# Attention in a fused two-layer kernel: lags between scores, transposed scores and weighted values, and the places of the work that rides along

## The chip, the cores and the metric

The kernel runs on one core of one Trainium2 chip. The time is the device time of one execution in microseconds, as the median of several runs. A core has five engines with queues of their own: TensorE (PE in the profile; PEld are its weight loads), VectorE (DVE), ScalarE (ACT), GpSimd (POOL) and SyncE (SP, which here only issues DMAs). Each queue is worked off in the order in which it was written, and engines wait for one another by semaphores.

## The reference, cut to what matters

The reference is two transformer-like layers over x of shape 2 x 512 x 512. Layer 0 is an attention of 32 heads (8 groups of keys and values, 4 heads to a group, head size 16) behind a modulated layer norm, then a gated low-rank feed-forward part; layer 1 has weights in 4-bit codes with scales. The change touches the attention of layer 0 and what is computed beside it:

```python
k = jnp.repeat(k, NREP, axis=2)
v = jnp.repeat(v, NREP, axis=2)
scores = jnp.einsum('bihd,bjhd->bhij', q, k) * SCALE
scores = jnp.where(causal, scores, jnp.finfo(scores.dtype).min)
attn = jax.nn.softmax(scores, axis=-1)
out = jnp.einsum('bhij,bjhd->bihd', attn, v)
```

and, of layer 1, the decoding of the weights, `w = NF4[codes]`, multiplied by a scale for each block of 64; q, k and v of layer 1 are added, so that one sum of three decoded matrices is needed.

## The kernel before

**Attention.** A unit is one tile of 128 queries for the 4 heads of one group: B x GROUPS x TB = 64 units, four to a group (unit n is tile n % 4 of group n // 4), and because of the causal mask the tiles need 1, 2, 3 and 4 blocks of 128 keys. For each unit:

- `scores(n)` (TensorE, L1607 and the mask L1609): two pairs of heads into PSUM banks 0 to 3. There is one set of these banks, so a pair is written only when the maxima of the same pair of the unit before were taken (semaphore `s_mx`).
- the maxima (VectorE, `reduce_max`, L1295) into one of two tiles of `MX`; a tile is overwritten only when GpSimd has used it (`s_dg`).
- the diagonal (GpSimd, L731): the maxima times an identity, written under the queries in the stack `QS`, so that the next product subtracts them.
- `transposed(n)` (TensorE, L1622, mask L1625): the scores again, keys on the partitions, less the maxima, one matmul per key block, into three banks in turn. A block needs the exponential of the third block before it.
- the exponential (ScalarE, L879) into ten tiles `PT`.
- `weighted(n)` (TensorE, L1639): the values and the denominators into bank 7, 4 matmuls per block, in pairs of units.

`scores(n)`, `transposed(n - 2)` and, at odd n, `weighted` of units n - 5 and n - 4 stand in one loop over n. When a group is complete, its bank 7 is copied by ScalarE (`copy_even`, L566) for even groups and by VectorE (`copy_odd`, L1215 and L1217) for odd ones. Each pair of groups is then finished on VectorE: `swap_sums` (L1223), two halves of a reciprocal (`invert`, L1227) and `divide` (L1232); ScalarE rounds the heads (`round_heads`) and VectorE splits them (`split_heads`, L1239).

**Work that rides along.** During attention six pieces of layer 1's codes are decoded. A piece has four steps, placed on units by `step_at(n)`: in each eight units the slots 2, 4 and 6. Steps 0 to 2 are curves on ScalarE (L837, four for a piece: two at step 0) and a sum on VectorE (L1157); step 3 is the `fold` on ScalarE (L846). ScalarE does the curves three units ahead of their slot (`ride(n + 3)`), the fold at it. GpSimd then scales the piece in two halves (`scale_half`, L687) one and two units behind the fold's unit, and adds it (`add_half`, L701) three and four units behind.

**SyncE's queue** (`load_stack`, L552 and L558): for each group twelve DMAs bring queries and keys into one of three stacks, each set behind a wait for the last transposed scores of the third group before. `load_piece` (codes L494, scales L503) stands between them, at groups 0, 5, 8, 11 and 14. The order of all this is written out by hand in the tables at the top of the file.

## Time and profile before

| what | us |
|---|---|
| median of 3 runs (952.17 to 954.70) | 953.95 |
| the profiled execution, its own time | 952.0 |
| its span from the first to the last instruction | 950.1 |
| TensorE busy | 877.9 (92%) |
| VectorE busy | 693.6 (73%) |
| ScalarE busy | 533.1 (56%) |
| GpSimd busy | 189.5 (20%) |
| mean granted TensorE clock | 0.976 of full speed |

The span is that of the profiled execution; its own time has the start and the end around it as well. Busy shares are means over stages with different limits, so the stage of the change has to be read by itself. In a row, "idle before" is the time in which an engine did nothing just before an instruction, and behind the arrow stands what ended it. Starts of TensorE's instructions are recorded and their ends are modelled, so durations are best read from one start to the next.

### The profile page before, as it was taken

The numbers are of one execution on the slowest core, as the hardware profiler recorded it, in microseconds if no ns is written. First come the engines' busy times: TensorE is split into PE (matmuls) and PEld (weight loads), VectorE is DVE, ScalarE is ACT, GpSimd is POOL, SyncE is SP. The second block draws the span as 40 slices with busy tenths as digits, with TensorE's granted clock in tenths as the row PEclk, the third lists the DMA queues.
The fourth block names the chain that finished last, engine by engine and source line by source line (L and its number), as shares of the span: only waits on it lengthen the run. The fifth ranks groups of instructions, "written<-read, shape, count | busy, mean of one in ns | idle before, by whom it ended". The sixth has DMA issues, their size and how long they took to land.

```text
span 950.1 us, 13799 instructions
## 1 busy us (share of the span) xinstructions
PE 877.9 (92%) x5224; PEld 693.3 (73%) x5224; DVE 693.6 (73%) x892; ACT 533.1 (56%) x707; POOL 189.5 (20%) x197
## 2 busy tenths in 40 slices
PE   2799999999988889898999999999988999999996
PEld 1567667666667668686888888788866888888885
DVE  3835698888888768778677777587887866667842
ACT  3313667657654434486666657477727766666830
POOL 3002555666557213300000000000040000000004
PEclk9798999999898999999999999999999999999998
DMA  9588565655535103105233333133312333332202
GB/s 309 171 243 152 67 109 69 113 101 66 103 78 179 34 12 105 51 22 147 83 106 103 102 99 113 46 105 95 111 45 67 111 104 97 99 101 67 67 1 89
DMA packets 40610, 93.59 MB, mean 99 GB/s; under 512 B 7000, under 2 KB 10072, under 8 KB 40544
## 3 DMA queue, kind: packets, MB, share of 16 engines
q1 hardware_dynamic: 36416, 87.35, 36.6%
q10 hardware_dynamic: 4128, 5.36, 1.7%
q8 instruction: 42, 0.69, 0.3%
q14 instruction: 24, 0.20, 0.1%
HBM read 77.98 MB, written 2.11 MB: 84 GB/s over the span
## 4 chain that ended last, share of the span: by engine, by line
PE 75%; DVE 9%; issue 5%; POOL 4%; ACT 3%; DMA 2%; SPq 1%; POOLq 0%; DVEq 0%; ACTq 0%
PE PS L1509 15%; PE PS L1510 14%; PE PS L1511 14%; PE PS L1815 5%; PE PS L1814 5%; PE PS L1813 5%; PE PS L1607 4%; PE PS L1639 2%; PE PS L1622 2%; DVE MX L1295 2%; POOL QS L731 2%; DMA WM<-in_WM 1%; POOL X L715 1%; PE PS L1531 1%; DVE ACC L1157 1%
## 5 line engine op out<-in xcount | busy, mean ns | idle before, releaser
L837 ACT ACTIVATE PL<-CODE 128x1024 f32<-128x1024 int32 x200 | 201.9, 1057 | 60.3 <-DVE ACC L1157 55.7
L1509 PE MATMUL PS<-HH,WRH 128*128 128x512 f32 x448 | 176.7, 394 | 11.2 <-DVE HL L1116 4.7
L1510 PE MATMUL PS<-HH,WRL 128*128 128x512 f32 x448 | 175.6, 392 | 0.0
L1511 PE MATMUL PS<-HL,WRH 128*128 128x512 f32 x448 | 175.6, 392 | 0.0
L715 POOL TENSOR_TENSOR X<-X,SCR 128x512 f32<-128x512 f32 x32 | 42.6, 1343 | 560.2 <-DVE SCR L1142 560.1
L1157 DVE SCALAR_TENSOR_TENSOR ACC<-PL,ACC 128x1024 f32<-128x1024 f32 x100 | 123.1, 1231 | 8.4
L879 ACT ACTIVATE PT<-PS 128x512 f32<-128x512 f32 x160 | 85.5, 602 | 67.3 <-PE PS L1622 45.1
L1295 DVE TENSOR_REDUCE MX<-PS 128x2 f32<-128x256 f32 (+3 forms) x128 | 100.5, 820 | 29.4 <-PE PS L1609 14.8
L1509 PEld LDWEIGHTS PS<-HH,WRH 128*128 128x128 f32 x448 | 84.9, 189 | 31.2 <-issue 6.3
L731 POOL TENSOR_TENSOR QS<-ident,MX 64x256 fp32r<-64x256 f32 x128 | 93.6, 732 | 66.6 <-DVE MX L1295 60.0
L1511 PEld LDWEIGHTS PS<-HL,WRH 128*128 128x128 f32 x448 | 84.8, 189 | 18.0
L1510 PEld LDWEIGHTS PS<-HH,WRL 128*128 128x128 f32 x448 | 85.0, 190 | 17.0
L1607 PE MATMUL PS<-KS,QS 128*128 128x128 f32 (+3 forms) x256 | 83.5, 387 | 7.8 <-DVE MX L1295 5.9
L1451 DVE TENSOR_TENSOR HID<-SG,PS 128x512 f32<-128x512 f32 x56 | 37.2, 684 | 69.1 <-PE PS L1511 44.6
L1813 PE MATMUL PS<-WRH,HH 128*128 128x512 f32 x216 | 84.1, 389 | 0.0
L1815 PE MATMUL PS<-WRH,HL 128*128 128x512 f32 x216 | 84.0, 389 | 0.0
L1814 PE MATMUL PS<-WRL,HH 128*128 128x512 f32 x216 | 84.0, 389 | 0.0
L1607 PEld LDWEIGHTS PS<-KS,QS 128*128 128x128 f32 x256 | 50.3, 196 | 30.0 <-DVE MX L1295 18.6
L1157 DVE SCALAR_TENSOR_TENSOR ACC<-PL 128x1024 f32<-128x1024 f32 x50 | 61.5, 1229 | 11.4 <-ACT PL L837 11.3
L846 ACT ACTIVATE ACC<-ACC 128x1024 f32<-128x1024 f32 x50 | 52.9, 1058 | 29.7 <-DVE ACC L1157 29.7
L1622 PE MATMUL PS<-QS,KN 128*128 128x512 f32 x160 | 57.1, 439 | 13.2 <-ACT PT L879 8.2
L1609 PE MATMUL PS<-maskR,padR 128*128 128x128 f32 x256 | 59.1, 240 | 0.0
(225 smaller groups left out, 1528.2 us busy)
## 6 DMA issues: line engine op xcount, KB each, us to landing
CODE<-in_CODES SPq DMA_DIRECT2D x50, 512.0 KB, 3.5
SCALE<-in_SCALES SPq DMA_DIRECT2D x100, 256.0 KB, 4.0
WM<-in_WM SPq DMA_DIRECT2D x12, 1024.0 KB, 5.9
QS<-FH SPq DMA_DIRECT2D x32, 128.0 KB, 4.1
QS<-FL SPq DMA_DIRECT2D x32, 128.0 KB, 5.1
X<-in_X ACTq DMA_DIRECT2D x2, 1024.0 KB, 12.3
GAB<-gates SPq DMA_DIRECT2D x4, 512.0 KB, 3.8
out_x<-X ACTq DMA_DIRECT2D x8, 256.0 KB, 2.0
```

The lines of the kernel that those rows point to most:

```text
L731: nc.gpsimd.tensor_tensor(QS[64:P, q % STACKS, :, ic * P + 64 * half:ic * P + 64 * half + 64], ident[rows, rows].unsqueeze(1).to_broadcast ...
L837: nc.scalar.activation(PL[:, n % 3], CODE[:, p % 2], ACT.Prelu, scale=scale, bias=bias, alpha=alpha).then_inc(s_plane, 1)
L879: nc.scalar.activation(block_of(n, jc)[:].rearrange("p h i -> p (h i)"), PS[:, 4 + done % 3], ACT.Exp, scale=HD ** -0.5).then_inc(s_exp, 1)
L1157: nc.vector.scalar_tensor_tensor(acc, PL[:, at_plane % 3], CAPS[i], rest_of, ALU.min, ALU.add).then_inc(s_used, 1)
L1295: nc.vector.reduce_max(MX[:, n % 2, 2 * pair:2 * pair + 2], PS[:, 2 * pair:2 * pair + 2, 0:w], AX_X).then_inc(s_mx, 1)
L1509: nc.tensor.matmul(dst, lh, rh, start=start and k == 0, stop=False)
L1510: nc.tensor.matmul(dst, ll, rh, start=False, stop=False)
L1511: ins = nc.tensor.matmul(dst, lh, rl, start=False, stop=stop and k == KC - 1)
L1607: nc.tensor.matmul(PS[:, h, 0:(ic + 1) * P], QS[:, q % STACKS, h, ic * P:(ic + 1) * P], KS[:, q % STACKS, 0:(ic + 1) * P], start=True, sto ...
L1813: nc.tensor.matmul(dst[t], hh, wh, start=(n == 1 and k == 0), stop=False, skip_group_check=True)
L1814: nc.tensor.matmul(dst[t], hh, wl, start=False, stop=False, skip_group_check=True)
L1815: ins = nc.tensor.matmul(dst[t], hl, wh, start=False, stop=last and n == 1, skip_group_check=True)
```

## The change

It changes places, not work. The transposed scores follow the scores by three units (`TURN`) instead of two, the weighted values of two units by six and five, at even n. The maxima have three tiles instead of two. The slots of the decoding are 0, 2 and 4 instead of 2, 4 and 6. On ScalarE a curve is done alone, five units (the first of a piece: seven) ahead of its slot, and the fold one unit behind it, all behind the unit's exponentials and ahead of the copy of an even group. GpSimd's scale halves come five and six units behind the fold's slot, its sums seven and eight. The copies, the swap, the inversions and the division on VectorE move to other units. Codes and scales are loaded at tables of their own.

```diff
-PIECES_AT = {0: (0, 1), 5: (2,), 8: (3,), 11: (4,), 14: (5,)}
+CODES_AT = {0: (0, 1), 4: (2,), 6: (3,), 9: (4,), 11: (5,)}
+SCALES_AT = {0: (0, 1), 5: (2,), 8: (3,), 11: (4,), 14: (5,)}
+MAXIMA = 3
+TURN = 3
-ROUND_AT = {41: 0, 46: 1, 49: 2, 54: 3, 58: 4, 60: 5, 63: 6}
+ROUND_AT = {41: 0, 46: 1, 49: 2, 54: 3, 58: 4, 61: 5, 63: 6}
...
-    slots = (2, 4, 6)
+    slots = (0, 2, 4)
...
-                    scale_at[n + 1 + half] = p, half
+                    scale_at[n + 5 + half] = p, half
-                        add_at[(n + 3 if p < 4 else B * GROUPS * TB - 3) + half] = p, half
+                        add_at[(n + 7 if p < 4 else B * GROUPS * TB - 3) + half] = p, half
...
-                if step_at(n) and step_at(n)[1] < STEPS - 1:
-                    curves(*step_at(n))
+                if step_at(n + 7) and step_at(n + 7)[1] == 0:
+                    curve(step_at(n + 7)[0], 0)
+                if step_at(n + 5) and step_at(n + 5)[1] < STEPS - 1:
+                    p, s = step_at(n + 5)
+                    curve(p, s + 1)
+                if step_at(n - 1) and step_at(n - 1)[1] == STEPS - 1:
+                    fold(step_at(n - 1)[0])
-            for n in range(3):
+            for n in range(-7, 0):
                 ride(n)
...
+                ride(n)
                 if n % 8 == 5:
                     copy_even(act, n // TB - 1)
-                ride(n + 3)
-                if step_at(n) and step_at(n)[1] == STEPS - 1:
-                    fold(step_at(n)[0])
...
-                    if n >= 2:
-                        dve.wait_ge(s_dg, 2 * (n - 1))
+                    if n >= MAXIMA:
+                        dve.wait_ge(s_dg, 2 * (n - MAXIMA + 1))
...
-                if pair_at(n, 4) is not None:
-                    copy_odd(pair_at(n, 4))
                 if pair_at(n, 5) is not None:
-                    swap_sums(pair_at(n, 5))
-                for half, unit in enumerate((5, 6) if n >= 60 else (7, 8)):
+                    copy_odd(pair_at(n, 5))
+                if pair_at(n, 14) is not None:
+                    divide(pair_at(n, 14))
+                if pair_at(n, 6) is not None:
+                    swap_sums(pair_at(n, 6))
+                for half, unit in enumerate((6, 7) if n >= 62 else (8, 12)):
                     if pair_at(n, unit) is not None:
                         invert(half)
-                if pair_at(n, 7 if n >= 60 else 9) is not None:
-                    divide(pair_at(n, 7 if n >= 60 else 9))
+                if n == B * GROUPS * TB - 1:
+                    divide(B * PAIRS - 2)
...
-            for n in range(units + 4):
+            for n in range(units + TURN + 2):
                 if n < units:
                     scores(n)
-                if 2 <= n < units + 2:
-                    transposed(n - 2)
-                if n >= 5 and n % 2 == 1:
-                    for unit in (n - 5, n - 4):
+                if TURN <= n < units + TURN:
+                    transposed(n - TURN)
+                if n >= 2 * TURN and n % 2 == 0:
+                    for unit in (n - 2 * TURN, n - 2 * TURN + 1):
                         weighted(unit)
```

`pair_at(n, unit)` gives pair p at unit 8 (p + 1) + unit.

What stands in a row on TensorE around the last unit of a group, before. Score matmuls read KS and QS and are as wide as the unit's keys (512 for the last tile, 128 for the first), transposed ones read QS and KN, weighted ones PT and V:

```order
L1607 MATMUL PS<-KS,QS 128x512
L1609 MATMUL PS<-maskR,padR 128x128
L1622 MATMUL PS<-QS,KN_90 128x512 x2
L1625 MATMUL PS<-padR,maskR 128x512
L1639 MATMUL PS<-PT_96,V 32x128 x4
L1639 MATMUL PS<-PT_97,V 32x128 x4
L1639 MATMUL PS<-PT_98,V 32x128 x4
L1639 MATMUL PS<-PT_99,V 32x128 x4
L1639 MATMUL PS<-PT_100,V 32x128 x4
L1639 MATMUL PS<-PT_101,V 32x128 x4
L1639 MATMUL PS<-PT_102,V 32x128 x4
L1607 MATMUL PS<-KS,QS 128x128
```

The same place in the changed kernel (its lines are numbered some ten higher):

```order
L1617 MATMUL PS<-KS,QS 128x512
L1619 MATMUL PS<-maskR,padR 128x128
L1632 MATMUL PS<-QS,KN_90 128x512
L1635 MATMUL PS<-padR,maskR 128x512
L1617 MATMUL PS<-KS,QS 128x128
L1619 MATMUL PS<-maskR,padR 128x128
```

Between the last scores of a group and the first of the next stood two transposed blocks and seven weighted ones; now one transposed block stands there, and the weighted blocks have moved behind the first scores of the next group and its two transposed blocks.

GpSimd's queue from the first diagonal on, before (two QS rows are one unit):

```order
L731 TENSOR_TENSOR QS<-ident,MX 64x4x64 x24
L687 TENSOR_TENSOR WT_104<-ACC,SCALE 128x512
L731 TENSOR_TENSOR QS<-ident,MX 64x4x64 x2
L687 TENSOR_TENSOR WT_104<-ACC,SCALE 128x512
L731 TENSOR_TENSOR QS<-ident,MX 64x4x64 x18
```

and in the changed kernel:

```order
L736 TENSOR_TENSOR QS<-ident,MX 64x4x64 x28
L692 TENSOR_TENSOR WT_104<-ACC,SCALE 128x512
L736 TENSOR_TENSOR QS<-ident,MX 64x4x64 x2
L692 TENSOR_TENSOR WT_104<-ACC,SCALE 128x512
L736 TENSOR_TENSOR QS<-ident,MX 64x4x64 x18
```

The first scale half has moved from behind unit 11 to behind unit 13, while the fold that it waits for has moved from slot unit 10 to 8.

## Rows read from the trace of the kernel before

**Rows 1.** Windows: busy us (instructions) of each engine, granted clock, DMA share, GB/s.
```profile
83.90:102.60 18.70, 16.48 (x97) 13.40 (x97) 14.41 (x20) 10.50 (x15) 9.41 (x12) 0.82 0.58 79
102.60:277.60 175.00, 161.58 (x1766) 121.20 (x1765) 148.30 (x180) 110.16 (x186) 101.27 (x127) 0.98 0.56 89
277.60:293.40 15.80, 11.78 (x156) 8.54 (x156) 11.36 (x8) 9.14 (x14) 11.37 (x9) 0.78 0.43 120
```

**Rows 2.** Timeline of TensorE, units 28 to 31: start, us, instruction [idle before].
```profile
166.21 0.33 PE L1607 MATMUL PS<-KS,QS 128*128 128x128 f32 x1
...
167.15 0.91 PE L1622 MATMUL PS<-QS,KN 128*128 128x512 f32 x3
...
170.20 0.50 PE L1622 MATMUL PS<-QS,KN 128*128 128x512 f32 x1 [0.28 <-ACT PT L879]
...
170.85 0.86 PE L1639 MATMUL PS<-PT,V 128*32 128x128 f32 x24
171.64 0.44 PE L1607 MATMUL PS<-KS,QS 128*128 128x384 f32 x1
...
172.85 0.45 PE L1622 MATMUL PS<-QS,KN 128*128 128x512 f32 x1
...
173.54 0.51 PE L1607 MATMUL PS<-KS,QS 128*128 128x512 f32 x1
...
174.41 0.50 PE L1607 MATMUL PS<-KS,QS 128*128 128x512 f32 x1
...
175.15 0.68 PE L1622 MATMUL PS<-QS,KN 128*128 128x512 f32 x2
...
175.99 1.74 PE L1639 MATMUL PS<-PT,V 128*32 128x128 f32 x56
177.66 0.33 PE L1607 MATMUL PS<-KS,QS 128*128 128x128 f32 x1
```

**Rows 3.** Timelines of ScalarE, GpSimd and TensorE around a scale half.
```profile
121.07 1.07 ACT L846 ACTIVATE ACC<-ACC 128x1024 f32<-128x1024 f32 x1
122.28 1.27 POOL L687 TENSOR_TENSOR WT<-ACC,SCALE 128x512 f32<-128x512 f32 x1 [3.52 <-issue]
128.68 0.70 PE L1622 MATMUL PS<-QS,KN 128*128 128x512 f32 x2 [0.83 <-POOL QS L731]
```

**Rows 4.** Timelines of ScalarE and TensorE, and a window, around unit 56.
```profile
248.22 2.01 ACT L837 ACTIVATE PL<-CODE 128x1024 f32<-128x1024 int32 x2 [2.10 <-DMA CODE<-in_CODES]
253.44 0.30 PE L1607 MATMUL PS<-KS,QS 128*128 128x128 f32 x1 [1.20 <-DVE MX L1295]
254.50:263.00 8.50, 8.20 (x48) 5.69 (x49) 5.89 (x7) 5.21 (x9) 5.43 (x8) 0.60 0.09 19
```

**Rows 5.** VectorE: timeline of units 30, 31; groups of 102 to 278 us.
```profile
172.53 4.32 DVE L1295 TENSOR_REDUCE MX<-PS 128x2 f32<-128x768 f32 x4 [0.32 <-DVE DENS L1223]
...
L1295 DVE TENSOR_REDUCE MX<-PS 128x2 f32<-128x1024 f32 x28 | 32.9, 1217 | 1.6 <-POOL QS L731 1.2
L1227 DVE RECIPROCAL DENS<-DENS 128x256 f32<-128x256 f32 x13 | 22.7, 1743 | 0.0
L1157 DVE SCALAR_TENSOR_TENSOR ACC<-PL,ACC 128x1024 f32<-128x1024 f32 x11 | 13.7, 1243 | 0.0
L1215 DVE SCALAR_TENSOR_TENSOR NUM<-PS,HALVES,NUM 128x512 f32<-128x512 f32 x7 | 5.2, 743 | 0.0
L1239 DVE TENSOR_TENSOR FL<-NUM,FH 128x512 fp32r<-128x512 f32 x4 | 3.1, 787 | 0.0
```

**Rows 6.** TensorE's wait behind unit 63, and ScalarE's exponentials, 102 to 278 us.
```profile
287.85 0.79 PE L1622 MATMUL PS<-QS,KN 128*128 128x512 f32 x1 [2.58 <-ACT PT L879]
...
L879 ACT ACTIVATE PT<-PS 128x512 f32<-128x512 f32 x141 | 75.3, 602 | 57.2 <-PE PS L1622 38.6 <-PE PS L1625 18.0
```

**Rows 7.** Timeline of GpSimd: two diagonals each, units 28 and 29.
```profile
166.44 1.30 POOL L731 TENSOR_TENSOR QS<-ident,MX 64x256 fp32r<-64x256 f32 x2 [1.25 <-DVE MX L1295]
167.92 2.15 POOL L731 TENSOR_TENSOR QS<-ident,MX 64x256 fp32r<-64x256 f32 x2 [0.19 <-DVE MX L1295]
```

More of the change, by code:

```diff
@@ L249, in build @@
         GAB = sb("GAB", [P, B, D], F32)
+        MX = sb("MX", [P, MAXIMA, REP], F32, gab0)
         MCOL = sb("MCOL", [P, 2, 4, KC, B], F32)
@@ L262, in build @@
         SD = sb("SD", [P, NT], F32)
-        MX = sb("MX", [P, 2, REP], F32)
         HALF = sb("HALF", [P, 2, 4], F32)
@@ L628, in _ @@
                         sp.dma_start(GD[:, b], MR[b:P:32]).then_inc(s_gd, 16)
-                for p in PIECES_AT.get(n, ()):
-                    load_piece(sp, p)
+                for p in CODES_AT.get(n, ()):
+                    load_codes(sp, p)
+                for p in SCALES_AT.get(n, ()):
+                    load_scales(sp, p)
             sp.wait_ge(s_used, len(CAPS) * N_QKV)
@@ L732, in _ @@
                                             ident[rows, rows].unsqueeze(1).to_broadcast([64, REP, 64]),
-                                            MX[rows, n % 2].unsqueeze(2).to_broadcast([64, REP, 64]), ALU.mult
+                                            MX[rows, n % MAXIMA].unsqueeze(2).to_broadcast([64, REP, 64]), ALU.mult
                                             ).then_inc(s_dg, 1)
@@ L1291, in _ @@
                     dve.wait_ge(s_s, 2 * n + pair + 1)
-                    if n >= 2:
-                        dve.wait_ge(s_dg, 2 * (n - 1))
+                    if n >= MAXIMA:
+                        dve.wait_ge(s_dg, 2 * (n - MAXIMA + 1))
                     w = (n % TB + 1) * P
-                    nc.vector.reduce_max(MX[:, n % 2, 2 * pair:2 * pair + 2], PS[:, 2 * pair:2 * pair + 2, 0:w], AX_X
+                    nc.vector.reduce_max(MX[:, n % MAXIMA, 2 * pair:2 * pair + 2], PS[:, 2 * pair:2 * pair + 2, 0:w], AX_X
                                          ).then_inc(s_mx, 1)
```

## The prediction

> **What bounds the kernel now.** I read the windows first. The change lies in the attention stage, about 84 to 293 us, so the stage stands in three pieces: units 0 to 6, units 7 to 62, and from unit 63 to the output projection [rows 1]. A unit is one tile of 128 queries of one group; four units are one group, which needs 1, 2, 3 and 4 key blocks. In the middle piece TensorE is busy 161.58 of 175.00 us, VectorE 148.30, ScalarE 110.16, GpSimd 101.27. So TensorE is the bound, VectorE close behind, and the most that the stage can give is TensorE's idle time, some 13 us there and some 4 us behind it. After the stage TensorE goes on without a gap, so what the stage wins or loses the kernel wins or loses.
>
> Next TensorE's own timeline of one quiet group, units 28 to 31 [rows 2]. Call scores S, transposed scores T, weighted values W, each with the unit's place 0 to 3 in its group. The starts give S0 0.94 us, T2 with S1 and T3 3.70 (0.28 of it a wait for an exponential), W0 and W1 0.79, S2 1.21, T0 0.69, S3 1.61, T1 0.84, W2 and W3 1.67: in all 11.45. Fourteen such groups are 160.3 us; the middle piece took 175.0. The 14.7 us above that are the disturbed groups. Two kinds explain most of it:
> - GpSimd's first half of a scaled weight piece starts 3.52 us after its last work, just behind ScalarE's fold, which ended at 122.14; TensorE then waits 0.83 us for GpSimd [rows 3]. GpSimd's queue is in order, so the diagonal of the next maxima stands behind a fold that ScalarE does late. Four more pieces repeat this.
> - ScalarE waits 2.10 us for codes, TensorE then 1.20 us for maxima, and behind that wait, from 254.5 to 263 us, its granted clock is 0.60 on average, that is mostly 1.2 instead of 2.4 GHz [rows 4]: 8.5 x 0.40 = 3.4 us lost.
>
> **The change, part by part.** The number of matmuls, maxima, exponentials, curves and divisions stays; only their places move.
>
> *GpSimd and codes.* The scale halves stand at five and six units behind the fold step instead of one and two, and the fold one unit behind it. ScalarE is then done before GpSimd comes. The codes of the later pieces are issued up to three groups earlier. The three tiles of maxima let VectorE run three units ahead of the diagonals, and T is three units behind S. I take both kinds of disturbance as gone: all 14.7 us. Of that, the late code load and the low clock are one group; it is gone if nothing else idles TensorE as long.
>
> *A new wait.* Before, S3 is followed by T1 and W2, W3: 2.51 us of cover before the next S0 writes the same four banks. Now the order is S3, T0, S0. The banks are free only when the maxima of S3 are read. In the quiet group VectorE's four reductions of units 30 and 31 run from 172.53 to 176.85 without a gap; one 1024-wide reduction takes 32.9/28 = 1.18 us [rows 5]. So behind S3's start (173.54) the first pair is free at 3.31 - 1.18 = 2.13 us and the second at 3.31. TensorE is done with S3 and T0 at 1.61 + 0.69 - 0.20 = 2.10, where 0.20 are small waits of S3 and T0 on unit 2's maxima (0.13: the first two heads take 0.87, the other two 0.74; and some 0.07 in T0), which go, since T3 and W now stand between S2 and S3. Then S0's first pair runs from about 2.2 to 2.7, the second starts at 3.36 and ends at 3.81, where 2.10 + 0.94 = 3.04 would be without the wait. That is +0.75 a group (bounds: 0, if VectorE got to S3's first pair earlier than this row shows; 1.2, if it is a whole reduction late). A group: 11.45 - 0.20 + 0.75 = 12.0, so 14 are 168.0, against 175.0: **-7.0**.
>
> *VectorE's chain.* In units 4 to 6 of each eight it now has the reductions, a curve sum 1.24, a reciprocal 1.74, the two copies of the odd group (0.74 each, row NUM) and the division with the swap (I take 0.74 each as well). I walked it from S3: maxima of unit 3 end at 3.3, unit 4 with sum and reciprocal at 7.4, unit 5 with copies at 10.0, unit 6 with division and swap at 13.2, where the reduction of unit 7 can start at 13.1. So it just fits, and each further piece there delays the next group. The three late splits of heads (units 46, 51, 54) do: 3 x 0.79 = 2.4 [rows 5]. At unit 29 ScalarE has a curve beside its fold (1.07) and the copies of an even group; its exponentials come about 1 us late; two roundings of heads cost some 0.3 each. Together **+4.0** (bounds 0 and 8). Elsewhere ScalarE's single curves stand behind a unit's exponentials, where 2 us or more are free: nothing; if that cover is gone, 1.07 each.
>
> *Start and end.* In units 0 to 6 VectorE is the bound (14.41 busy of 18.70 us, with the gate values). It gets one more sum there, 1.24, and T0 moves to where unit 3's maxima are waited for: **+1.4** (0 to 3). At the end T60 stands behind S63, so ScalarE has one more exponential ahead of the last four, 75.3/141 = 0.53, where TensorE already waits 2.58 us for it [rows 6]: **+0.6** (-2 to +2; minus if the clock, 0.78 on average in that piece, stays up).
>
> *SyncE's queue.* A stack load waits for a T that now comes one unit later, two to four us, and is needed six units on instead of seven. The codes' four DMAs stand ahead of later stacks, the scales where they were; none adds a byte. I cost this at nothing: the view of waits names no DMA that TensorE waited for in the middle piece. If that cover is gone, a late stack costs up to the same two to four us, once a group.
>
> **A rule weighed.** VectorE's sums and divisions read two tensors of SBUF while GpSimd writes diagonals. In this trace GpSimd is the one that gives way: two diagonals take 2.15 us where a sum runs and 1.30 where none does [rows 7], and the 11 two-input sums kept 1.24. So I add nothing. The Trainium skill (SBUF — State Buffer, Who interferes with whom) says that whoever issues first holds the pair for its whole instruction and the other fully blocks; By it alone the sum would gain rival 3's price wherever GpSimd's moved halves come first.
>
> **Sum.** -7.0 + 4.0 + 1.4 + 0.6 = -1.0 us. The profiled execution took 952.0 (span 950.1), so it would be 951.0; the median of the three is 953.95, and I forecast **953.0**. About 0.3%, 2.9 us, is what a measurement of this kernel can tell from no change; the forecast is inside. Its own range is 950 to 956.
>
> **Rivals.**
> 1. *Faster: the new wait is mostly hidden.* If VectorE, relieved of sums before the last unit of a group, has S0's banks free half as late (0.35 a group less, -4.9) and half of the collisions don't occur (-2), the time is 946. For it: VectorE idles 26.7 us in the middle piece, some of it just before unit 2's maxima. Against it: the 3.31 us of rows 5 are a gapless pair of reductions, and no cover is left between S3 and S0.
> 2. *Slower: the clock falls.* The new wait, with a split on top (0.75 + 0.79), is over 1.5 us, more than the 1.20 us behind which the clock fell at 254 us [rows 4]. If it falls twice (units 48 and 56), where the forecast has no fall, that is 2 x 3.4 = +6.8, so 960. It decides from the point where a wait at S0 passes about 1.2 us. Against it: the waits of 0.83 [rows 3] left no mark on the clock, whose mean over the middle piece is 0.98 with the one fall in it [rows 1], and TensorE is busy some 90% of each new group. The Trainium skill (TensorE: Matmul & The Clock Gate, The HAM clock gate) says that the throttled state is the default and that activity releases it; by that rule more small idles speak against this change, and the sum would be rival 2's.
> 3. *Slower or faster through the shared port:* if each of the 16 scale and add halves held back VectorE by half its 1.28 us, (0.64), that is up to +10, and about half of it would be covered where the chain has slack: 958. Rows 7 speak against it.
> 4. *It does nothing:* the stalls are replaced one by one, time 954.
>
> **Chances.** Forecast 0.46 (0.10 of it beyond -0.3%, 0.02 beyond +0.3%), rival 1 0.27, rival 2 0.15, rival 3 0.08, rival 4 0.04. So faster 0.37, same 0.38, slower 0.25. The range: rival 1 with no wait at all and no collisions would be 939, which I leave out; its middle down to 944.5 and rival 2 up to 961 are in.
>
> **What would show it.** Right: GpSimd's 3.5 us gaps before its scale halves and ScalarE's wait for codes are gone; TensorE's waits are named after the maxima and sit in the second half of each S0, about 0.65 us in each group, with starts of like units 12.0 us apart; at units 48 and 56 it is over 1 us. Wrong: groups of 11.4 us (rival 1), stretches at 0.50 of the clock between 110 and 270 us (rival 2), VectorE's sums over 1.4 us (rival 3), or TensorE waiting for ScalarE's exponentials more than 0.28 us a group, which would make the single curves the bound.

## The result, and the profile after

| | before | changed |
|---|---|---|
| median of the runs, same chip in turn | 950.77 us (20 runs, 949.49 to 954.70) | 955.86 us (20 runs, 953.22 to 958.01) |
| ratio, 95% interval | | 1.0044 [1.0033, 1.0055] |
| the profiled execution | 952.0, span 950.1 | 955.9, span 954.1 |

The change makes the kernel slower by 0.44%, some 4 us: the ratio of the runs gives 4.2, the two profiled executions 3.9, the two medians alone 5.1. The forecast was 953.0, no change, with 0.25 on slower; the time lies inside the range of 944.5 to 961. The kernel before took 953.95 in the three runs from which the forecast started and 950.77 in twenty, so 953.0 is nearer to 955.86 than the forecast change is to the measured one (-0.95 against +4.2); that nearness is luck.

The windows of the changed kernel, cut at the same events as in [rows 1] (S0, S7, S63, first output projection):

```profile
84.50:105.80 21.30, 17.16 (x95) 13.79 (x95) 16.39 (x21) 10.77 (x16) 11.47 (x14) 0.76 0.39 52
105.80:281.60 175.80, 160.33 (x1768) 122.20 (x1765) 146.86 (x175) 109.38 (x184) 102.13 (x126) 0.98 0.56 90
281.60:297.20 15.60, 12.48 (x162) 8.92 (x158) 14.12 (x12) 10.02 (x16) 11.07 (x9) 0.80 0.42 117
```

By the starts of those instructions the stage is 2.7 us longer at its start (21.28 against 18.62), 0.8 longer in the middle (175.84 against 175.02) and as long at its end (15.76 against 15.82); 0.5 more lies ahead of S0, which the change doesn't touch. 2.7 + 0.8 - 0.1 + 0.5 = 3.9, and the span grew by 4.0. The middle was to lose 3 us.

TensorE's timeline of the group of units 28 to 31, as [rows 2]:

```profile
168.98 0.30 PE L1617 MATMUL PS<-KS,QS 128*128 128x128 f32 x1 [0.21 <-DVE MX L1303]
...
170.02 0.33 PE L1617 MATMUL PS<-KS,QS 128*128 128x128 f32 x1 [0.41 <-DVE MX L1303]
...
170.52 0.68 PE L1632 MATMUL PS<-QS,KN 128*128 128x512 f32 x2
...
171.36 1.74 PE L1649 MATMUL PS<-PT,V 128*32 128x128 f32 x56
173.02 0.39 PE L1617 MATMUL PS<-KS,QS 128*128 128x256 f32 x1
...
177.27 0.50 PE L1632 MATMUL PS<-QS,KN 128*128 128x512 f32 x1 [0.28 <-ACT PT L889]
...
178.73 0.50 PE L1617 MATMUL PS<-KS,QS 128*128 128x512 f32 x1
...
180.15 0.45 PE L1632 MATMUL PS<-QS,KN 128*128 128x512 f32 x1
...
181.09 0.30 PE L1617 MATMUL PS<-KS,QS 128*128 128x128 f32 x1 [0.26 <-DVE MX L1303]
```

S0 now waits twice for the maxima of S3, 0.21 us for the first pair of heads and 0.41 for the second, and from S0 to S0 the group takes 12.11 us instead of 11.45. The waits that the changed order was to remove are gone. GpSimd's first scale half starts with no idle time ahead of it (3.52 in [rows 3]), and so does ScalarE's first curve of a late piece (2.10 in [rows 4]):

```profile
127.69 1.27 POOL L692 TENSOR_TENSOR WT<-ACC,SCALE 128x512 f32<-128x512 f32 x1
```

So in the middle piece TensorE waits for two things alone. The view of its waits, of which the columns are the total, the number and the longest:

```profile
PE PS L1617 <- DVE MX L1303: 11.6, 28, 1.3
PE PS L1632 <- ACT PT L889: 3.6, 13, 0.3
```

The 1.3 us are S48 and S56, where a split of heads stands ahead of the maxima. Timeline, and windows from there on:

```profile
231.00 0.30 PE L1617 MATMUL PS<-KS,QS 128*128 128x128 f32 x1 [1.32 <-DVE MX L1303]
...
258.21 0.30 PE L1617 MATMUL PS<-KS,QS 128*128 128x128 f32 x1 [1.33 <-DVE MX L1303]
```

```profile
231.00:233.00 2.00, 1.59 (x10) 1.41 (x11) 1.57 (x3) 0.00 (x0) 0.80 (x2) 0.97 0.93 99
233.00:236.60 3.60, 3.60 (x58) 2.59 (x57) 3.17 (x3) 2.14 (x3) 3.36 (x4) 0.54 0.39 65
...
258.20:263.80 5.60, 5.19 (x67) 3.94 (x67) 4.75 (x5) 2.14 (x3) 4.15 (x5) 0.70 0.55 75
```

Behind each the granted clock (the third number from the end) goes to half, 0.54 and 0.70 on average. The starts give 13.63 us for the group of unit 48 and 13.64 for that of unit 56. At the start of the stage the longest wait is S4's, 1.76 us behind the gate's values (VectorE L1086 to L1089, 95.23 to 98.07), again with a low clock behind it:

```profile
98.54 0.38 PE L1617 MATMUL PS<-KS,QS 128*128 128x256 f32 x1 [1.76 <-DVE MX L1303]
```

```profile
98.00:104.00 6.00, 5.46 (x23) 4.69 (x23) 4.76 (x8) 2.04 (x4) 3.29 (x4) 0.72 0.00 0
```

The groups of VectorE's work in the middle piece, as [rows 5]. The maxima and the reciprocals cost what they did, the sums of curves more, 1442 ns instead of 1243:

```profile
L1303 DVE TENSOR_REDUCE MX<-PS 128x2 f32<-128x1024 f32 x28 | 32.9, 1218 | 12.0 <-PE PS L1619 11.0 <-DVE DENS L1231 0.9
...
L1235 DVE RECIPROCAL DENS<-DENS 128x256 f32<-128x256 f32 x12 | 20.9, 1740 | 0.0
...
L1165 DVE SCALAR_TENSOR_TENSOR ACC<-PL,ACC 128x1024 f32<-128x1024 f32 x10 | 14.4, 1442 | 0.0
```

### The profile page after: what moved, and what is told of

Its sections match the earlier page's. It is cut to its first block, busy times and chain, and to the rows that moved or that the text cites. A ratio compares the mean times of both kernels' runs of the same rounds, so it can differ in the third digit from the quotient of the medians.

```text
span 954.1 us, 13799 instructions
## 1 busy us (share of the span) xinstructions
PE 877.1 (92%) x5224; PEld 694.7 (73%) x5224; DVE 696.9 (73%) x892; ACT 533.5 (56%) x707; POOL 192.1 (20%) x197
## 4 chain that ended last, share of the span: by engine, by line
PE 68%; DVE 8%; ACT 4%; issue 4%; POOL 2%; DMA 1%; POOLq 0%; SPq 0%; DVEq 0%; ACTq 0%
PE PS L1519 13%; PE PS L1520 13%; PE PS L1521 13%; PE PS L1825 5%; PE PS L1823 5%; PE PS L1824 5%; PE PS L1649 3%; PE PS L1617 2%; DVE MX L1303 2%; PE PS L1632 2%; ACT PT L889 1%; POOL X L720 1%; DVE ACC L1165 1%; PE PS L1806 1%; PE PS L1619 1%
## 6 DMA issues: line engine op xcount, KB each, us to landing
X<-in_X ACTq DMA_DIRECT2D x2, 1024.0 KB, 12.3
```

## The experiments

Twelve runs. All times are medians; "ratio to before" compares with the kernel before, run beside them on the same chip, 952.2 to 952.3 us. Beside the changed kernel it took 950.77, so a difference of a median to 955.86 carries 1.5 us of doubt; the ratios and the pieces are the safer numbers. The pieces come from TensorE's starts in each profile:

| run | time, us | ratio to before | S0 to S7 | S7 to S63 |
|---|---|---|---|---|
| before | | | 18.62 | 175.02 |
| changed | 955.86 | 1.0044 [1.0033, 1.0055] | 21.28 | 175.84 |
| a_tfirst | 949.14 | 0.9964 [0.9951, 0.9978] | 21.23 | 169.06 |
| a_split | 951.54 | 0.9990 [0.9978, 1.0002] | 21.27 | 171.15 |
| b_pool | 949.03 | 0.9967 [0.9954, 0.9980] | 17.34 | 173.12 |
| b_codes | 949.50 | 0.9971 [0.9958, 0.9983] | 18.35 | 172.29 |
| c_gate | 952.68 | 1.0000 [0.9988, 1.0012] | 19.80 | 174.96 |
| c_tfinv | 942.26 | 0.9890 [0.9874, 0.9906] | 21.28 | 163.11 |
| c_ball | 948.71 | 0.9964 [0.9950, 0.9978] | 15.54 | 173.26 |
| c_best | 938.05 | 0.9853 [0.9837, 0.9870] | 17.45 | 162.93 |
| d_again | 955.23 | 1.0026 [1.0013, 1.0039] | 21.26 | 175.80 |
| d_bboth | 948.10 | 0.9948 [0.9933, 0.9963] | 18.33 | 169.53 |
| d_back | 950.31 | 0.9976 [0.9964, 0.9989] | 17.84 | 171.09 |
| d_max2 | 939.88 | 0.9864 [0.9847, 0.9881] | 18.09 | 162.93 |

S0 itself comes between 83.0 and 85.7 us, and from the first output projection to the end it is 655.7 to 659.2 us; nearly all of that code is the same in all these kernels. Some 2 us of a difference in the time can come from there, so the pieces are read beside the medians.

The theory behind the first four runs: the reordering leaves S0 uncovered behind S3's maxima (some 0.6 us a group), two splits bring that over 1.3 us and the clock falls, and GpSimd's and ScalarE's housekeeping is a gain that the reordering eats up. The rival: what is slower is VectorE's chain as a whole, or the housekeeping gained nothing.

### a_tfirst: T1 between S3 and the next S0

```diff
+                first = n % TB == 0
+                if first and TURN <= n < units + TURN:
+                    transposed(n - TURN)
                 if n < units:
                     scores(n)
-                if TURN <= n < units + TURN:
+                if not first and TURN <= n < units + TURN:
                     transposed(n - TURN)
```

> The changed kernel with one edit: in the first unit of each group TensorE does the transposed scores ahead of the scores. Theory A (the missing cover between the last scores of a group and the first of the next is the main cost): the waits for maxima at each S0 (0.2 + 0.4 us, with some 0.2 us more of idle that is not named) are gone, a quiet group takes 11.4 to 11.5 us instead of 12.1, 15 groups give 9 to 10 us, and the clock no longer falls in units 48 and 56 (1.6 us each), so the kernel takes 944 to 947 us where the changed kernel took 955.9. Theory B (VectorE's chain of reductions, reciprocals and copies is the bound, the wait at S0 only its sign): the wait moves to another unit, groups stay at 12.0 to 12.1 us and the time within 1.5 us of the changed kernel's.

Measured: 949.14 us, 6.7 less than the changed kernel, where 944 to 947 us was expected; the middle piece lost 6.8. T1's two blocks, exchanged with the scores at one unit in four, cover S0. No wait of the middle piece is over 0.87 us and its clock stays up, so 3.0 of the 6.8 are the two falls (a_split, next), and the rest is cover. In a group without a sum of curves S0 waits 0.23 us (second pair) and S0 to S0 is 11.30 us, less than the 11.45 of [rows 2]. In a group with one it is mostly 12.14 to 12.45, since the wait moved to S2:

```profile
179.07 0.33 PE L1617 MATMUL PS<-KS,QS 128*128 128x128 f32 x1 [0.23 <-DVE MX L1303]
...
183.98 0.44 PE L1617 MATMUL PS<-KS,QS 128*128 128x384 f32 x1 [0.54 <-DVE MX L1303]
```

VectorE at that place shows why. The sum (which I had at 1.24) and the inversion stand back to back in the group's shortest unit. The change itself put them together: before, the sums stood at places 2, 4 and 6 of each eight units and the inversions at 7 and 0, now the sums stand at 0, 2 and 4 and the inversions at 0 and 4.

```profile
180.11 1.43 DVE L1165 SCALAR_TENSOR_TENSOR ACC<-PL 128x1024 f32<-128x1024 f32 x1
181.46 1.74 DVE L1235 RECIPROCAL DENS<-DENS 128x256 f32<-128x256 f32 x1
```

### a_split: the two splits away from the unit before an S0

```diff
-SPLIT_AT = {46: 0, 51: 1, 54: 2, 59: 3}
+SPLIT_AT = {49: 0, 51: 1, 57: 2, 59: 3}
```

> The changed kernel with one edit: the splits of heads 0 and 2 on VectorE at units 49 and 57 instead of 46 and 54. Theory C (the two falls of the clock come from the waits of 1.3 us at units 48 and 56, and these from the split that stands at the end of VectorE's full stretch): the named waits at units 48 and 56 go back to 0.2 us, the clock stays at 1.00 from 230 to 290 us, and the kernel is 4 to 5 us faster than the changed one, at 951 to 952. Rival (the clock falls through the sum of the small idles in each group, whatever the splits do): the waits shrink by 1.1 us each, the clock falls somewhere in the stage all the same, and the gain is 0 to 2.2 us.

Measured: 951.54 us, 4.3 less than the changed kernel. The waits at S48 and S56 fall to half a microsecond (0.51 and 0.53) and the clock stays up in both groups, which take 12.14 us instead of 13.6:

```profile
229.72 0.30 PE L1617 MATMUL PS<-KS,QS 128*128 128x128 f32 x1 [0.51 <-DVE MX L1303]
```

So each split cost 0.8 us as a wait (1.32 - 0.51) and 1.5 as a low clock: 2 x 2.3 = 4.6, and the middle piece gave 4.7.

### b_pool and b_codes: the housekeeping alone, in the order before

```diff
-                    scale_at[n + 1 + half] = p, half
+                    scale_at[n + 5 + half] = p, half
-                        add_at[(n + 3 if p < 4 else B * GROUPS * TB - 3) + half] = p, half
+                        add_at[(n + 7 if p < 4 else B * GROUPS * TB - 3) + half] = p, half
```

> The kernel before with one edit: GpSimd's scale halves five and six units behind the fold's slot instead of one and two, its sums seven and eight. If the 3.5 us gaps in GpSimd's queue cost TensorE what the disturbed groups show (groups 3, 6, 8, 9, 11 and 13 are 0.4 to 2.0 us over 11.45, 8 us in all): 943 to 946 us against 950.8 before. If other waits take their place (VectorE's two tiles of maxima, exponentials behind curves), 948 to 950.

Measured: 949.03 us; 943 to 946 was expected, and 948 to 950 if other waits took the place of those removed. In the middle piece it gives 1.9. The groups at units 12 and 32 go from 13.07 and 13.40 to 12.01 each, that at 36 from 12.72 to 11.69, but those at 40 and 48 go up, from 11.89 to 12.84 and from 11.97 to 12.80, and the group at 56 stays at 14.99, since ScalarE still waits for codes. Another 1.3 us of the gain lie in S0 to S7, ahead of the first unit that the edit touches: there the clock did not fall (1.00 from 83 to 98 us), where in the kernel before it is low from 85 to 92.

```diff
-PIECES_AT = {0: (0, 1), 5: (2,), 8: (3,), 11: (4,), 14: (5,)}
+CODES_AT = {0: (0, 1), 4: (2,), 6: (3,), 9: (4,), 11: (5,)}
+SCALES_AT = {0: (0, 1), 5: (2,), 8: (3,), 11: (4,), 14: (5,)}
```

> The kernel before with one edit: codes of pieces 2 to 5 loaded at groups 4, 6, 9 and 11, scales where they were. If ScalarE's wait of 2.1 us for codes is what brought the late group 14 its wait and its low clock (15.1 us instead of 11.45), the gain is 3 to 5 us: 946 to 948. If it is only a sign, under 1 us.

`load_piece` is nothing but `load_codes` and `load_scales`, which are now called by a table each.

Measured: 949.50 us, where 946 to 948 was expected. The group at 56 goes from 15.10 to 12.81 with no low clock in it, and the middle piece gives 2.7. Both housekeeping parts were gains, so the loss lies in the rest of the change, the new order and the places that moved with it.

### c_gate: the gate's values at unit 6

```diff
-                if n == TB - 1:
+                if n == 6:
                     gate_values()
```

> The changed kernel with the gate's values at unit 6 instead of unit 3. It asks what undersized the term of the start (S0 to S7 21.28 us measured, 20.0 in the sum). Theory A (the gate's values, 2.9 us of VectorE between unit 3's maxima and unit 4's, make S4 wait 1.76 us at 98.54, and the clock falls in 98 to 104 behind it): that wait goes, the granted clock stays over 0.9 in 94 to 104, S7 comes 1.5 to 2.5 us earlier, and if the values then hold S7 or S8 by no more than 0.5, the time is 953.5 to 954.5. Rival B (the values only move: VectorE is 2.9 us behind wherever they stand in the short units, so S7 or S8 waits as long): S8 comes at the same time within 0.5 us, and the time is 955.5 to 956.5. Rival C (the clock falls at the start whatever S4 waits, behind the idle pieces of units 0 to 2): S4's wait goes (-1.3) but the clock reads 0.5 to 0.7 again in 94 to 104, time 954.5 to 955.5.

Measured: 952.68 us. S4's wait of 1.76 is gone, but TensorE's clock is at half from 86 to 100 us all the same, and S8 now waits 0.88 us. From S0 to S8 it takes 22.79 us against 23.59 (22.76 in the kernel before): 0.8 gained, which is rival C's mechanism, though its time was 954.5 to 955.5. The rest is not the gate's: 1.5 of it is a fall that did not come. At S48 the clock did not fall, though the wait was as long as in the changed kernel:

```profile
230.64 0.30 PE L1617 MATMUL PS<-KS,QS 128*128 128x128 f32 x1 [1.33 <-DVE MX L1303]
```

```profile
232.60:236.60 4.00, 4.00 (x71) 3.11 (x70) 3.97 (x5) 3.71 (x6) 3.77 (x4) 1.00 0.38 62
```

That group took 12.14 us. At S56 a wait of 1.32 was followed by a low clock again (13.62 us).

### d_again: the changed kernel once more

No edit.

> The changed kernel once more, unaltered, for a second profile. It asks whether the clock's late falls belong to the waits at S0 or to the moment. In the first profile the clock fell behind both waits of 1.3 us (231.00 and 258.21); in the run with the gate's values at unit 6 two waits as long (230.64, 256.35) were followed by one fall. Theory A (each wait of 1.3 us with 0.4 behind it brings the fall): falls behind both again, groups at 48 and 56 of 13.6 us, time 955 to 956.5. Rival B (the wait is needed but where it falls against the clock's own rhythm decides): the same two waits of 1.3 us, but 0, 1 or 2 falls, each fall 1.5 us of the group, time 952.5 to 956.5. Rival C (the falls need no such wait): a fall in a group whose S0 waits 0.7 or less.

Measured: 955.23 us, and the same falls at the same places, groups of 13.65 us at units 48 and 56:

```profile
232.80:236.40 3.60, 3.60 (x58) 2.58 (x57) 3.17 (x3) 2.14 (x3) 3.37 (x4) 0.53 0.40 66
258.00:263.70 5.70, 5.28 (x68) 3.99 (x68) 4.77 (x5) 2.08 (x3) 4.24 (x5) 0.70 0.57 74
```

So this program repeats its falls; yet c_gate lost one of them. Its TensorE is the same there: from S8 to S48 it takes 122.92 us in c_gate (107.72 to 230.64), 122.94 in the changed kernel (108.06 to 231.00) and 122.88 here (107.92 to 230.80), no unit of these forty starts more than 0.04 us off that even distance, and the wait is 1.33, 1.32 and 1.32. What differs is that all of it comes earlier in c_gate, by 0.35 us against the changed kernel and by 0.2 against this run. Theory A's numbers came true here and its rule did not hold in c_gate, which leaves rival B's, that the moment counts too. The ratio here is 1.0026 against 1.0044 in the twenty runs, so the loss is between 2.5 and 4.2 us.

### c_tfinv: T1 ahead of S0, inversions away from the sums

```diff
-                for half, unit in enumerate((6, 7) if n >= 62 else (8, 12)):
+                for half, unit in enumerate((6, 7) if n >= 62 else (9, 11)):
```

and the edit of a_tfirst.

> As the run with transposed scores ahead of the scores at each group's first unit (949.1 us), and the inversions of a pair at units 9 and 11 instead of 8 and 12, so that neither stands in the unit of a curve's sum. Theory A (what is left in the groups that have a curve's sum, 12.15 to 12.45 us against 11.3 without, is VectorE's own chain at units 0 to 2 and 4 to 6: maxima 2 x 1.2, the curve's sum 1.24 and the inversion 1.74 together hold S2): the groups at units 16, 20, 24, 32 and 36 fall from 12.15-12.44 to 11.3-11.6, some seven groups by 0.7 to 0.9, time 942.5 to 945. Rival B (the curve's sum alone holds them, the inversion counts for nothing): groups stay within 0.2 us, time 948.5 to 950. Rival C (the inversion moved to unit 9 or 11 holds that unit's copies and the wait moves to S2 or S4 of the next): the 12.2 groups fall but those at 11.3 rise to 12, time 947 to 950.

Measured: 942.26 us, 6.9 less than a_tfirst, of which the middle piece holds 5.9 (163.11 against 169.06). Groups with a sum of curves, 12.14 to 12.45 up to unit 39, are at 11.36 to 11.82, and those without stayed at 11.3. VectorE's work is the same, but no unit holds a sum and an inversion at once. Theory A.

### c_ball and d_bboth: do the housekeeping gains add?

c_ball is b_pool, b_codes and the gate's edit together; d_bboth leaves the gate's values at unit 3.

> The kernel before with three small edits together: GpSimd's scale halves and adds four units later (alone 949.0 against 952.3 before), ScalarE's code loads a unit or two earlier (alone 949.5), and the gate's values at unit 6. If the two gains lie in different groups (the GpSimd stalls of 3.5 us at units 8 to 39, the code wait in the group at unit 52 to 56) they add: -3.2 -2.8, and with the gate's values 0 to -2: 944.5 to 946.5. If the group at 56 takes its 15 us from both (it stayed 14.99 with the GpSimd part alone and went to 12.81 with the codes alone) the gains add all the same. Rival: both free the same wait by delaying the same unit (the clock's fall at units 56 to 58), then the time is 948 to 949.

> The kernel before with GpSimd's scale halves and adds four units later (alone 949.0 beside 952.3) and the code loads earlier (alone 949.5); the gate's values stay at unit 3. It asks whether these two gains add, which the run with the gate's values too (948.7) left open, since there S8 waited 2.00 us and the group at 8 took 13.17. Theory A (they lie at different units and add, the gate's values at unit 6 cost 1.7 to 2 us in this order): 945.5 to 947. Rival B (they free the same low clock at units 56 to 59, so together they give little over one): 948 to 949.3. In the run of all three the groups from 8 to 59 took 157.8 us against 159.73 with GpSimd's part alone, of which 2.2 lie in the group at 56; by that I expect 946.5 to 947.5.

Measured: 948.71 and 948.10. Both times are those of the rivals, by which the two edits free the same wait, and not those that I expected; but the rivals' mechanism isn't what happened. In the middle piece the two gains do add: d_bboth's 169.53 is 5.5 us under the kernel before, more than 1.9 + 2.7. The group at 52 makes the difference: 12.73 before, 13.00 and 12.28 with one part, 11.61 with both; that at 56 is at 12.80, as with b_codes alone. Of these 5.5 the time shows some 4; in this profile the way from the first output projection to the end is 1.6 us longer than before (658.3 against 656.7), and why is open. In c_ball the gate's values hold up S8, and the clock falls behind it:

```profile
107.16 0.30 PE L1610 MATMUL PS<-KS,QS 128*128 128x128 f32 x1 [2.00 <-DVE MX L1298]
```

Its group at unit 8 takes 13.17 us against 11.41 in d_bboth. From S0 to S12 it took 34.90 us against 33.87 in d_bboth, so in the order before the gate's edit costs 1.0; in the changed one it gave 0.8 (34.85 against 35.65). In the expectation of c_ball I had kept the clock out of it once more.

### c_best: all four repairs

The edits of a_tfirst, a_split, c_gate and the inversions at 9 and 11, on the changed kernel.

> The changed kernel with four edits: transposed scores ahead of the scores at a group's first unit (alone -6.8), splits at 49 and 57 (alone -4.3), inversions at units 9 and 11, and the gate's values at unit 6. By the theory that S0's wait behind VectorE's maxima is the one wait that the change put on TensorE's path, that the clock's two late falls follow it, and that VectorE's chain at a curve's sum is what is left: groups at 11.3 to 11.6 throughout but 44 to 59 (12.3), start 1.5 us shorter: 938.5 to 942. By the rival that the gains overlap (the splits' gain is gone once S0 does not wait, the inversions only shift the wait): 945 to 949.

Measured: 938.05 us, ratio 0.9853 [0.9837, 0.9870]: 14 us faster than the kernel before and 18 than the changed one. The windows of its middle and its waits there:

```profile
101.00:264.00 163.00, 153.82 (x1769) 122.99 (x1765) 146.82 (x178) 107.94 (x184) 102.62 (x127) 1.00 0.59 97
```

```profile
PE PS L1617 <- DVE MX L1303: 5.2, 18, 0.4
PE PS L1632 <- ACT PT L889: 3.9, 14, 0.3
```

TensorE is busy 94% of it at full clock and no wait is over 0.4 us; the 3.9 us are the fourth block of a group's T3, which waits 0.28 for an exponential. From unit 8 to unit 51 all groups take 11.3 to 11.8 us. The middle piece took the same in c_tfinv (163.11), so c_best's gain over it lies at the start, where S0 to S7 takes 17.45 instead of 21.28, with the clock at half for some 3 us instead of 13 (two windows of 2 us at 0.53 and 0.61, against eight below 0.9). How much of that is the gate's edit and how much the moment is not told apart.

### d_back: the best version with GpSimd's halves put back

```diff
-                    scale_at[n + 5 + half] = p, half
+                    scale_at[n + 2 + half] = p, half
-                        add_at[(n + 7 if p < 4 else B * GROUPS * TB - 3) + half] = p, half
+                        add_at[(n + 4 if p < 4 else B * GROUPS * TB - 3) + half] = p, half
```

Two units behind the slot is right behind the fold, which itself is a unit later than before.

> The best version so far (938.05 us: changed kernel, transposed scores first at a group's first unit, splits at 49 and 57, inversions at 9 and 11, gate's values at 6) with GpSimd's scale halves put back to right behind the fold (two and three units behind the slot, sums four and five). Theory A (the halves stand in GpSimd's queue while ScalarE does the fold late, so the diagonals wait 3 us; three units of lag cover at most one of it): the 3 us gaps before GpSimd's halves come back, TensorE waits 0.3 to 0.8 us in some six groups, 940 to 942.5. Rival B (the three tiles of maxima and the third unit of lag cover the whole gap): gaps on GpSimd, none on TensorE, 937.5 to 938.7. Rival C (the halves are then still late enough, since ScalarE's fold is done by the start of the unit behind): no gaps at all, 938.

Measured: 950.31 us, 12.3 more than c_best, far over each theory's number. The middle piece grew by 8.2; of the rest, S0 comes 1.9 us later and the way from the first output projection to the end is 3.0 longer (659.2 against 656.2), and why is open. GpSimd waits for the fold with the next diagonals behind it, and TensorE for a diagonal:

```profile
151.27 1.26 POOL L692 TENSOR_TENSOR WT<-ACC,SCALE 128x512 f32<-128x512 f32 x1 [5.34 <-issue]
```

```profile
154.05 0.70 PE L1632 MATMUL PS<-QS,KN 128*128 128x512 f32 x2 [2.65 <-POOL QS L736]
...
252.65 0.70 PE L1632 MATMUL PS<-QS,KN 128*128 128x512 f32 x2 [2.95 <-POOL QS L736]
```

```profile
PE PS L1632 <- POOL QS L736: 7.6, 4, 3.0
```

These waits are 7.6 of the 8.2 us; the view counts four. With T three units behind S, ScalarE is three units behind too, so a fold behind a unit's exponentials comes a unit later for GpSimd, whose diagonals follow the maxima: gaps of 4.56, 5.34 and 5.64 us at three pieces instead of the 3.52 of [rows 3]. As I read it, the third unit of lag does not cover such a gap but makes it longer. The parts of the change belong together: the same placement is worth 1.9 us in the middle piece of the order before (b_pool), and 8.2 in the new one.

This run also has two waits longer than any above, with windows behind them:

```profile
154.00:158.50 4.50, 4.45 (x63) 4.07 (x67) 2.28 (x3) 2.03 (x3) 4.19 (x5) 0.69 0.49 72
...
252.60:257.00 4.40, 4.35 (x76) 3.98 (x76) 2.56 (x4) 2.87 (x5) 4.09 (x5) 1.00 0.39 60
```

Behind 2.65 us the clock fell, behind 2.95 it did not.

### d_max2: two tiles of maxima in the best version

```diff
-MAXIMA = 3
+MAXIMA = 2
```

> The best version so far (938.05 us) with two tiles of maxima instead of three. It asks whether the third tile is what lets VectorE run ahead. Theory A (VectorE's maxima of unit n wait for GpSimd's diagonal of n-2, which is done some 1 us behind the maxima of n-2, long before): no wait of VectorE for GpSimd over 0.3 us but where a scale half stands between, 938 to 939. Rival B (behind each scale half and sum of 1.3 us the diagonals come late and VectorE, the chain that holds S0, waits for them): waits of 0.3 to 1 us at some 16 halves, half of them on the path, 940 to 943.

Measured: 939.88 us, but the middle piece is 162.93 us in both, to the hundredth. VectorE does wait for GpSimd now, up to half a microsecond at a few units, and none of it reaches TensorE:

```profile
122.06 1.29 DVE L1303 TENSOR_REDUCE MX<-PS 128x2 f32<-128x512 f32 x2 [0.50 <-POOL QS L736]
```

In the profile S0 came 2.1 us later (85.69 against 83.59), ahead of any use of these tiles, which is more than the whole difference of the spans (937.2 and 935.7). I take the third tile as worth nothing here.

## Why the prediction was wrong

**The new wait: right, a little short.** The place (S0, behind the maxima of S3), the cause and the form (most of it at the second pair) were as told; the named waits are 0.21 + 0.41 = 0.62 where I had 0.75 less the end of the small ones. A quiet group came to 12.04 to 12.15 us, mostly 12.1, for 12.0. Over 14 groups that is 1.4 us too little.

**What was to go, went, but it was worth less.** GpSimd's gaps and the wait for codes are gone, and b_pool, b_codes and d_bboth show that they were worth 5.5 us of the middle piece. I had put all 14.7 us over fourteen quiet groups down to them; in d_bboth 9.2 of these are still there. Since S7 to S63 is 169.53 us with the two alone and 175.84 with the whole change, the rest of the change cost 6.3. That all groups but the disturbed ones came level at 12.1, so that my base of 14 x 12.0 held, is in part luck.

**VectorE's chain: right in place, undersized only through the clock.** I had 4.0 for splits and collisions. Against 12.1, the groups that end in the waits behind the splits are 1.2 us (unit 44) and 1.5 us (unit 52) longer, of which the split itself is 0.8 each by a_split; the groups at 20 and 36 are 0.35 longer each: 3.4. Unit 29 cost nothing that shows, its group is one of the quiet ones.

**The step that failed is the sum's clock.** I wrote that the low clock "is gone if nothing else idles TensorE as long", and in the same text put S0's wait with a split on top at over 1.5 us, over the 1.20 behind which it had fallen. Both can't stand in one sum: the wait that I had priced was the one that I had excluded. Rival 2 named the event, the units (48 and 56) and the number of falls rightly, with 0.15. Its size was too large, 3.4 a fall where the groups show 1.5 (13.63 against 12.14 in a_split), because the fall before lasted from 256 to 263 us, and these, at half for some 3 us each, were shorter. So: 168.0 + 1.4 + 3.4 + 3.0 = 175.8, the middle piece as measured, where I had 172.0. Against the sum's -1.0 us for the whole kernel, the profiled execution shows +3.9: 3.0 of the difference of 4.9 are the falls, 1.4 the wait at S0, -0.6 the chain, 1.3 the start, -0.7 the end, and 0.5 lies ahead of the stage.

**The start: 2.7 where I had 1.4.** My bounds were 0 to 3. I counted the extra sum, and not that the gate's values now fall between the maxima of unit 3, on which S4 depends, and those of S4 itself, with no T or W left to cover them. The price of the low clock there is settled only in part: b_pool, where it did not fall before S7, took 17.34 us for 18.62, while in c_gate, which took the wait away, the clock stayed low. By S8 the difference to before is 0.8 us, as the next unit takes 2.3 us instead of 4.1.

**The end: nothing where I had +0.6.** TensorE's wait of 2.58 [rows 6] has become two, in the same time:

```profile
288.52 1.47 PE L1632 MATMUL PS<-QS,KN 128*128 128x512 f32 x3 [1.33 <-ACT PT L889]
291.77 0.80 PE L1632 MATMUL PS<-QS,KN 128*128 128x512 f32 x1 [1.78 <-ACT PT L889]
```

**The rule weighed.** I added nothing for sums of VectorE beside GpSimd's work. That was wrong on the hardware and nearly right on the time. Of 15 sums in the middle piece nine took 1.43 us instead of 1.22, and the longest 1.86. The sum of unit 20, on VectorE, and the diagonal that GpSimd had begun before it:

```profile
146.45 1.43 DVE L1165 SCALAR_TENSOR_TENSOR ACC<-PL 128x1024 f32<-128x1024 f32 x1
```

```profile
146.19 0.61 POOL L736 TENSOR_TENSOR QS<-ident,MX 64x256 fp32r<-64x256 f32 x1
```

The diagonal has 0.35 us left when the sum begins, and the sum takes 0.21 longer than 1.22. I had named sums over 1.4 us as the sign of rival 3, and the sign is there at a third of the price (0.21 for 0.64). The longest one meets a half instead of a diagonal, and two more runs have such a meeting. The changed kernel, c_best and b_pool, in this order:

```profile
189.11 1.28 POOL L692 TENSOR_TENSOR ACC<-ACC,SCALE 128x512 f32<-128x512 f32 x1
189.62 1.86 DVE L1165 SCALAR_TENSOR_TENSOR ACC<-PL,ACC 128x1024 f32<-128x1024 f32 x1
```

```profile
186.24 1.27 POOL L706 TENSOR_TENSOR WT<-WT,ACC 128x512 f32<-128x512 f32 x1
186.97 1.63 DVE L1165 SCALAR_TENSOR_TENSOR ACC<-PL,ACC 128x1024 f32<-128x1024 f32 x1
```

```profile
194.76 1.28 POOL L701 TENSOR_TENSOR WT<-WT,ACC 128x512 f32<-128x512 f32 x1
194.78 2.33 DVE L1157 SCALAR_TENSOR_TENSOR ACC<-PL,ACC 128x1024 f32<-128x1024 f32 x1
```

The half has 0.77, 0.54 and 1.26 us left, and the sum takes 0.64, 0.41 and 1.11 longer: the rest of what GpSimd had begun, less some 0.14 us. By the Trainium skill (SBUF — State Buffer, Who interferes with whom) a VectorE instruction with two inputs in SBUF contends with a GpSimd instruction that reads SBUF, and the order of issue decides who blocks; that the other one blocks for the whole instruction is said there of VectorE's two-port modes. The rows here agree: the one that comes second waits for nearly the whole rest of the other. So what a sum pays hangs on how much of GpSimd's piece is left when the sum begins, and rival 3's price was too high because most sums met a short diagonal and not a half. In c_best six sums take 1.43 and its groups still come to 11.3 to 11.8, so the stretch lies in VectorE's free time there.

**The clock and small idles.** Where I weighed rival 2 I named small idles as what could bring the clock down. They did not: from 106 to 181 us the changed kernel has S0's 0.62 us in each group and a clock of 1.00 throughout:

```profile
106.00:181.00 75.00, 69.09 (x766) 52.74 (x765) 60.35 (x74) 46.83 (x79) 40.24 (x52) 1.00 0.60 95
```

The rule of the Trainium skill that I cited (TensorE: Matmul & The Clock Gate, The HAM clock gate), that activity releases the clock, bears on the two long waits and not on these.

## What to carry to other kernels

When an order is changed to hide a latency, ask of each buffer with one copy what now stands between its last reader's start and its next writer: here a lag of one more unit took the cover from the one place that needed it, and exchanging two calls at one unit in four gave it back, worth 6.7 us, 3 of it through the clock. Place long pieces of side work so that no short unit holds two of them (6.9 us for moving the inversions by a unit, 5.9 of it in the middle piece), and make the sum of a forecast pass its own test: a wait that it contains must also be charged for what such a wait did elsewhere in the trace. And a piece that was worth 2 us in one order can be worth 8 in another, so parts are to be tried in the order in which they will run.

## What the hardware showed that I had not expected

The clock. Behind waits of 1.20, 1.32, 1.33, 1.47, 1.76, 2.00 and 2.65 us the granted clock fell to half. Behind one of 1.33 at the same instruction (c_gate), one of 1.52 (d_back, at 190.99 us) and one of 2.95 (d_back) it stayed at full speed, and so it did behind S4's 1.52 to 1.54 in the kernel before, b_pool, b_codes and d_bboth. At S63 it fell behind 1.84 us (d_bboth) and stayed up behind 1.82 (c_ball). The same program repeated its falls to within 0.3 us (d_again). From unit 8 to the first output projection each fall had a wait of over 1.1 us ahead of it, and waits up to 1.05 us had none behind them, but above that the length alone doesn't decide. c_gate and the changed kernel come near to a test of what else does: forty units of TensorE's work and the wait at S48 are the same in both, 0.35 us apart in time, and one has the fall and the other not. So the moment of a wait counts; what sets the right moment is open.

Between VectorE and GpSimd the one that begins second gives way. In the kernel before most sums began 0.2 us ahead of a diagonal and kept their 1.22 us, and GpSimd's two diagonals took 2.15 us instead of 1.30 [rows 7]; after the change most sums began 0.27 us behind one and took 1.43. A half of GpSimd's takes 1.28 us, or 2.15 when a sum had begun. In the trace of the kernel before it looked as if only GpSimd gave way, because there the sums came first.

Not tried: a lag of two units with the rest of the best version. It needs another guard for the buffer that the rounded heads share with the stack loads. How much of the 12 us that the best version gains in the middle piece needs the third unit of lag is therefore open.
